# Constant matmuls on TensorE ahead of the softmax attention and between its first score tiles

## The reference, cut to what matters

```
q = embedded @ Wq.T + bq;  k = embedded @ Wk.T + bk;  v = embedded @ Wv.T + bv      # 16 heads of 8 numbers
qk = einsum('bhqd,bhkd->bhqk', q, k) / sqrt(s)
p  = softmax(qk, axis=-1) * triu(ones(s, s))        # the mask comes after the softmax
z  = einsum('bhqk,bhkd->bhqd', p, v)
out = layernorm(embedded + z) * gamma + beta
```

## Time and profile before

| | us |
|---|---|
| median of 3 runs | 879.61 (878.43 to 880.32) |
| the profiled execution, its own time | 876.03 |
| its span | 874.2 |
| mean granted clock of TensorE | 0.882 |
| busy: TensorE (PE) | 672.2 (77%) |
| busy: VectorE (DVE) | 580.9 (66%) |
| busy: ScalarE (ACT) | 455.2 (52%) |
| busy: GpSimd (POOL) | 332.0 (38%) |

### The profile page before, as it was taken

How to read it: one execution, slowest core, us unless ns; L and a number is a source line. 1 busy time by engine, 2 the same in 40 slices (tenths; PEclk the granted TensorE clock), 3 DMA queues, 4 the chain that set the end, 5 groups by cost and what they waited for, 6 DMA issues and landing times.

```text
span 874.2 us, 14331 instructions
## 1 busy us (share of the span) xinstructions
PE 672.2 (77%) x4582; PEld 347.0 (40%) x4582; DVE 580.9 (66%) x1141; ACT 455.2 (52%) x872; POOL 332.0 (38%) x767
## 2 busy tenths in 40 slices
PE   4185867545409946899999999999999999952993
PEld 4172322434408934123333434343333423421992
DVE  5436998825533448868788787879978797333343
ACT  2045501223106635047777677867767677851661
POOL 0634564255442423321433324144342344161342
PEclk9997999578558978559999999999999999985897
DMA  8352940044112014620010202020020000011103
GB/s 261 114 155 56 272 70 1 12 128 117 29 58 65 27 54 119 184 57 2 23 34 2 56 1 57 1 57 1 2 56 2 1 2 2 4 34 55 47 28 100
DMA packets 56929, 51.31 MB, mean 59 GB/s; under 512 B 6152, under 2 KB 46804, under 8 KB 56600
## 3 DMA queue, kind: packets, MB, share of 16 engines
q1 hardware_dynamic: 52168, 42.19, 18.7%
q0 software_dynamic: 4544, 7.60, 3.4%
q10 hardware_dynamic: 144, 0.61, 0.3%
HBM read 30.04 MB, written 21.80 MB: 59 GB/s over the span
## 4 chain that ended last, share of the span: by engine, by line
PE 55%; issue 17%; DVE 16%; DMA 5%; POOL 3%; ACT 2%; SPq 2%; POOLq 0%; ACTq 0%; DVEq 0%
PE PS L1080 14%; PE PS L1008 11%; PE PS L1047 11%; PE PS L785 6%; DVE ARENA L1821 6%; PE PS L796 5%; DVE X L1426 2%; DVE XN L1377 2%; DVE STATS L1350 2%; PE PS L757 1%; DMA ARENA<-slots_x 1%; PE PS L735 1%; PE PS L748 1%; POOL slots_x L1875 1%; SPq L541 1%
## 5 line engine op out<-in xcount | busy, mean ns | idle before, releaser
L1821 DVE TENSOR_REDUCE ARENA<-PS 128x1 f32<-128x1024 f32 x256 | 301.0, 1219 | 63.3 <-PE PS L1008 62.5
L1315 ACT ACTIVATE ARENA<-PS 128x512 f32<-128x512 f32 x512 | 273.0, 606 | 78.6 <-PE PS L1047 73.6
L1008 PE MATMUL PS<-ARENA 72*128 72x512 bf16 x512 | 165.5, 407 | 13.7 <-DMA ARENA<-k_parts 7.3
L1047 PE MATMUL PS<-ARENA 75*128 75x512 bf16 x512 | 163.4, 386 | 0.0
L1080 PE MATMUL PS<-ARENA 128*8 128x128 f32 (+8 forms) x1920 | 152.5, 432 | 1.2 <-POOL ARENA L1997 1.0
L1997 POOL TENSOR_SCALAR_AFFINE_SELECT ARENA<-ARENA 128x128 f32<-128x128 f32 x256 | 74.5, 298 | 127.9 <-ACT ARENA L1315 127.6
L1047 PEld LDWEIGHTS PS<-ARENA 75*128 75x128 bf16 x512 | 48.1, 98 | 88.5 <-ACT ARENA L1315 38.8
L1008 PEld LDWEIGHTS PS<-ARENA 72*128 72x128 bf16 x512 | 42.7, 100 | 99.2 <-DVE ARENA L1821 39.8
L1696 DVE TENSOR_TENSOR ARENA<-PS,ARENA 128x512 f32<-128x512 f32 x46 | 31.8, 692 | 68.0 <-PE PS L785 68.0
L1080 PEld LDWEIGHTS PS<-ARENA 128*32 128x32 f32 (+2 forms) x1920 | 43.4, 98 | 77.9 <-issue 43.1
L1905 POOL DMA_INDIRECT tokens_y<-ARENA x46 | 44.7, 972 | 74.9 <-DVE ARENA L1705 73.1
(11 more groups left out here) (188 smaller groups left out, 876.3 us busy)
## 6 DMA issues: line engine op xcount, KB each, us to landing
ARENA<-pack_dram SPq DMA_DIRECT2D x8, 514.0 KB, 13.2
ARENA<-slots_x SPq DMA_DIRECT2D x16, 256.0 KB, 3.8
slots_y<-ARENA SPq DMA_DIRECT2D x32, 128.0 KB, 2.9
ARENA<-q_parts SPq DMA_DIRECT2D x21, 192.0 KB
ARENA<-k_parts SPq DMA_DIRECT2D x21, 192.0 KB
slots_x<-FILL SPq DMA_DIRECT2D x2, 1483.5 KB, 19.5
ARENA<-slots_x SPq DMA_DIRECT2D x10, 258.0 KB, 5.4
k_parts<-ARENA SPq DMA_DIRECT2D x10, 256.0 KB, 3.4
```

The source lines that it names most:

```text
L1008: ins = nc.tensor.matmul(PS[:, slot + c, :], Q3[0:KQ, G % Q3R, g, i * P:(i + 1) * P], K3[0:KQ, G % Q3R, g, c * 512:(c + 1) * 512], start=T ...
L1047: nc.tensor.matmul(PS[:, bank, 0:w], K3[0:MR + 3, G % Q3R, i, j * P:(j + 1) * P], Q3[0:MR + 3, G % Q3R, i, half * 512:half * 512 + w], sta ...
L1315: nc.scalar.activation(PT[:, n % NPT, 0:w], PS[:, bank_of[x], 0:w], ACT.Exp).then_inc(b_exp, 1)
L1821: nc.vector.tensor_reduce(NM[:, k % 4, i:i + 1], PS[:, slot:slot + 2, :].rearrange("p b n -> p (b n)"), AX.X, ALU.max, negate=True).then_i ...
```

## The change

A helper, fill(bank, count), issues count matmuls of the identity by the first 256 columns of C, in float32, into a bank of PSUM, without a wait and without a signal. Nothing reads what they write. It is called in three places: 24 of them into bank 3 at the start of the soft stage, 12 into bank 3 behind the waits for qf_done and one8_made, and one into bank 7 behind every A tile that comes before the first B, 22 in all.

```diff
@@ -665,6 +665,11 @@
             ident = col("ident")
 
+            def fill(bank, count):
+
+                for _ in range(count):
+                    nc.tensor.matmul(PS[:, bank, 0:256], ident, C[:, 0:256], start=True, stop=True)
+
             def norm_turned(ln, kind, k):
@@ -942,6 +947,7 @@
                     i.then_inc(vproj_done, 1)
 
+                fill(3, 24)
                 turn(0)
                 turn(1)
@@ -956,6 +962,7 @@
                 pe.wait_ge(qf_done, 8)
                 pe.wait_ge(one8_made, 1)
+                fill(3, 12)
 
                 def wait_slot(n):
@@ -986,6 +993,7 @@
                 begun = set()
+                first_key_score = sum(x[0] == "A" for x in plan[:plan.index(("B", 0, 0))])
                 pe.wait_ge(v9_ready, 4)
@@ -1009,6 +1017,8 @@
                         ins.then_inc(a_scores, 1)
+                        if n < first_key_score:
+                            fill(7, 1)
                     elif kind == "M":
```

## The result

The changed kernel takes **872.3 us** (median of 11 runs, 868.72 to 874.82) against 878.43 (11 runs, 875.61 to 880.34): a ratio of 0.9931, 95% interval 0.991 to 0.9951. The prediction was 872.9. Run once more beside other kernels, the same change gave 0.9957 (0.9941 to 0.9974). So the two comparisons put its worth at 6.1 and 3.8 us, with intervals that reach from 2.3 to 7.9 together. All ratios leave out executions more than 1.5% above the fastest of their kernel; only the kernel with fills of 128 columns had any, three of twelve.

A forecast was written before the change was run, and what follows sets the result against it. VectorE was taken to bound the score tiles, and TensorE at half clock the stretch from 376 to 392. Terms 0 + 0 + 0 - 6.7 on 876.0 gave 869.3, plus 3.6 to the median: 872.9 us, range 869.0 to 880.0.

The forecast's parts named there:

- The 24 fills: Ahead of the transposes: 0.46 us each, over at 326.2, hidden with 1.2 us of cover; cost and gain taken as 0.
- The 12 fills: Ahead of the first score tile: cost 0 with 1.3 us of cover; first tile 0.60 in place of 1.03, -0.43 us.
- The 22 fills: One per score tile: 0.89 us of TensorE work within the 1.178 that VectorE needs, so hidden, 0.
- The mix: Work behind the score tiles at full clock: V's second product ends at 385.7, not 392.4; -6.7 us, first tile's 0.43 included.
- the step that says the profiled execution stands for all of them: Whole kernel: gain read from the profiled execution, 876.0 us, applied to the median, 879.6, keeping the 3.6 between them.
- The sum: Whole kernel: 0 + 0 + 0 - 6.7 on 876.0 gives 869.3; with the 3.6 to the median, 872.9 us.
- Does the clock hold: Score tiles and mix: granted clock stays 1.00 from 315 to 392 and beyond; the sum hangs on it.
- a clock that is full when it meets such work keeps its level: Argument for the tiles, from the steady mix: more than half bf16, yet it holds 1.00 for 40 us.
- The argument from the linear attention: From 88 to 138 the clock stayed 1.00 with TensorE some 57% busy; score tiles with fills would be 76% busy.
- The first (some tiles at half): Score tiles: clock goes to and fro, 4 to 11 of 22 tiles lose 0.59 each; 875.3 to 879.4 us; chance 0.15.
- The second (clock lost early and not regained): From the gap before the first tile or within the tiles: half clock stays, 13.0 us lost, 892.6; chance 0.13.
- The third: Clock full at 351.68 but lost before 376 or in the mix: time as before, 878 to 881 us; chance 0.06.

## Why the prediction was right, and where it was off

- **The 24 fills, taken as 0: right.** They alone gave 1.0008, and without them nothing was lost (0.9957 both ways). In the profile they end at 329.6 and the transposes wait 1.80 more. What they were to bring did not come there: the clock was not at 1.00 from 315 on, it fell behind them, and the first four projections took 4.73 against 4.22 before (3.68 when the change was run once more). Nothing was lost by that. That ScalarE and VectorE hold the chain there was the right reading of the earlier trace rows.
- **The 12 fills, taken as 0 with 0.43 gained: right in their cost, small in what they bring.** They end 1.52 before the first tile starts, 1.3 forecast. Without them two tiles ran at half clock, and the stretch was 1.2 longer, so in the profiles they are worth more than the 0.43, which counted the first tile alone; in the ratios neither shows. Their cover is also their weak point: a wait of 1.92 behind them cost 1.8 us once, and in two profiles of variants no cover was left.
- **The 22 fills, taken as hidden: right**, by the tiles 1.13 apart. But the bound that hid them was misread. "VectorE stays the bound and the 20 maxima still take 23.55" failed: at half clock it was the slot's turn, and at full clock the maxima took 1.135 each. The forecast has 24 maxima ahead of TensorE's own part; over these it is 24 x 0.043 = 1.0 us more gain than forecast.
- **The mix, taken as 6.7 in all: 7.4 between the two profiles**, and the step in it that was mis-sized is that 1.0; TensorE's own part took 388.98 - 383.63 = 5.35 where 5.13 were forecast, which takes 0.2 back. But the step that says the profiled execution stands for all of them was off in the other way. In three kernels without a fill in the tiles the stretch was 37.5 to 38.2, as the clock rose 35 us or so behind the first tile and not 40 as in the profile before, and 38.54 in a fourth; against 33.28 that is a gain of 4.2 to 5.3. The ratios (0.9931 and 0.9957, 6.1 and 3.8 us) go with such a mixture; what the stretch was in the executions without a profile is not known.
- **The sum: 872.9 for 872.3, and this near in part by luck.** The sum put the profiled execution at 869.3 and the median 3.6 above it. The change's profiled execution took 873.68, 1.4 above its median and 2.35, not 6.7, under the one before; a later start of the tiles and a fall of the clock near 640 stand between. The gain of the medians was 6.1 in the first comparison and 3.9 in the second. The mechanism is what the profiles bear out; the last digits are not.
- **Does the clock hold: yes.** All windows of the tiles are at 1.00. One argument for it was wrong: "a clock that is full when it meets such work keeps its level" does not hold in the tiles without fills, where the clock fell 4 to 5 us after the first tile. The argument from the linear attention stands. The Trainium skill's rule on kernels that idle briefly between matmuls ("TensorE: Matmul & The Clock Gate", A second HAM failure mode: psum-queue depth-cycling) describes those bare tiles better than I allowed, for the clock does fall there; it did not go to and fro, it fell once and stayed. In this case the measured runs decide: with fills of 256 columns it held in each of five profiles with one fill per tile in which the first tile met a full clock and TensorE had waited 1.52 us or less. (The 0.79 of the earlier trace rows for 330 to 332 is the mean clock of the window; the share of it at full is 0.58. The 330.8 follows from that.)
- **The rivals.** None came in the two profiles of the change. The first (some tiles at half) was seen once in a variant of it, at 1.8 us. The second (clock lost early and not regained) did not come with 256 columns and came once with 128. The third did not come.

## What to carry to other kernels

An engine that looks full at half clock is a hole: find where the granted clock falls, and ask which stretch behind it has TensorE alone on the chain, because only there is a full clock worth anything; here that were 16 us of 40 at half clock, and in the ffn1 stages nearly nothing. Filler must keep the clock through the stretch before that one, fit into the waits with room (one fill of 0.44 in 1.135 was hidden, two took the whole gain and more), and be large enough that the clock comes back if it was lost (256 columns were, 128 were not in the one profile that shows it). Look at the spread of the runs as well as at the median, and take the gain from more than one profile of the kernel before.

## What the runs showed of the hardware that was not expected

**The clock falls in the steady mix too.** The 1.4 us that the change's profile lost near 640 (windows of 1 us):

```profile
636.00:637.00 1.00, 0.42 (x12) 0.11 (x4) 0.96 (x4) 0.44 (x1) 1.00 (x5) 1.00 0.86 160
637.00:638.00 1.00, 0.41 (x8) 0.12 (x8) 1.00 (x2) 0.00 (x0) 0.89 (x5) 1.00 0.79 162
638.00:639.00 1.00, 0.66 (x3) 0.31 (x4) 1.00 (x2) 0.00 (x0) 0.87 (x4) 1.00 0.34 67
639.00:640.00 1.00, 1.00 (x5) 0.31 (x4) 1.00 (x4) 0.80 (x2) 0.13 (x1) 0.80 0.00 0
640.00:641.00 1.00, 1.00 (x6) 0.20 (x8) 1.00 (x3) 0.90 (x3) 0.61 (x3) 0.50 0.00 0
```

TensorE waits 0.68 us for GpSimd's mask and 0.83 for VectorE, and the clock is at half from 639.8 until 643. The profile before has the same two waits (0.68 and 0.84) three microseconds later, and no fall. Six of the 14 profiles show a fall between 635 and 655, with and without fills in the tiles; in two of them, the one with the 12 alone and the one with fills in ffn1 alone, it reached over three windows of 5 us. Part of the spread of all these kernels may come from there; no run tried to fill those waits.

**The way out of half clock depends on what runs.** From the first B on, bf16 of 72 and 75 rows with V's products kept TensorE busy without a gap and needed nine to fifteen microseconds (376.8 to 386.4 with the 24 alone, 377.2 to 392.1 before); tile and fill of 256 columns were at full clock again after two tiles in one run and four in another; tile and fill of 128 columns, as densely packed, not in the 28 us from 358 to 386.

**The same wait does not always cost the clock.** Ahead of the second four projections TensorE waited 2.64 us in the profile of the change run once more, and the granted clock stayed at 1.00; in the profile with two fills per tile it waited 2.65 us at the same place, behind the same work, and the clock fell within the wait, at 344.2, and rose again at 351.0. What decides between the two is not shown.
